# Routed pairs of a mixture-of-experts stage: both up halves ahead of the down product of the preceding pair, and VectorE's weighing behind both gated products

## What is computed

```python
def swiglu(x, w1, w2, w3):
    h = x @ w1
    return h * jax.nn.sigmoid(h) * (x @ w2) @ w3
...
top_v, top_i = jax.lax.top_k(gate_out, TOP_K)
...
out = jax.vmap(one_expert, in_axes=(0, 0, 0, 2))(ew1, ew2, ew3, w).sum(0)
out = out + swiglu(x, sw1, sw2, sw3)
...
h = h + _L0_ffn_ref(_layernorm(h, axis=-1), ...)
```

## Time and profile before

| | us |
|---|---|
| median of 3 runs (lowest to highest) | 1470.19 (1468.88 to 1470.64) |
| the profiled execution, its own time | 1476.68 |
| span of the profiled execution, first to last instruction | 1474.9 |
| PE busy in that span | 1277.8 (87%) |
| DVE busy | 1043.0 (71%) |
| ACT busy | 831.4 (56%) |
| POOL busy | 960.0 (65%) |

### The profile page before, as it was taken

The page is one execution under the profiler, slowest core; times in us unless marked ns, Lnnn a source line. Parts: engine busy times, 40 slices in busy tenths (PEclk is TensorE's granted clock), DMA queues, the critical chain, the costliest instruction groups (busy, mean ns, idle before and its releaser), DMA issues. The chain is left out here.

```text
span 1474.9 us, 37041 instructions
## 1 busy us (share of the span) xinstructions
PE 1277.8 (87%) x10992; PEld 1053.6 (71%) x10993; DVE 1043.0 (71%) x2675; ACT 831.4 (56%) x2286; POOL 960.0 (65%) x958
## 2 busy tenths in 40 slices
PE   4400499999999999999999999879989999999996
PEld 3400388888888888888888888645557888788884
DVE  3245789998998899899889999756564444444442
ACT  1230388778778877787787777765632322222221
POOL 0057789889889888988898889558640333333333
PEclk8755799999999999999999999979999999999998
DMA  9993264543463355346332546554433434444440
GB/s 320 380 319 118 47 127 102 138 87 69 102 133 64 64 131 108 64 89 142 70 65 58 116 87 107 97 84 127 128 125 102 67 54 58 70 57 58 63 60 8
DMA packets 354415, 157.13 MB, mean 107 GB/s; under 512 B 283953, under 2 KB 338737, under 8 KB 354353
## 3 DMA queue, kind: packets, MB, share of 16 engines
q1 hardware_dynamic: 321090, 117.99, 35.8%
q0 software_dynamic: 20064, 25.32, 9.3%
q10 hardware_dynamic: 13200, 13.11, 2.5%
HBM read 44.50 MB, written 42.64 MB: 59 GB/s over the span
## 5 line engine op out<-in xcount | busy, mean ns | idle before, releaser
L731 PE MATMUL bank<-hT,Wc 128*128 128x256 f16 x2304 | 285.8, 274 | 88.0 <-DMA hT<-hhl 76.0
L731 PEld LDWEIGHTS bank<-hT,Wc 128*128 128x128 f16 x2304 | 226.7, 98 | 115.9 <-issue 88.5
L691 POOL DMA_INDIRECT out_rows<-h0b,payin x78 | 121.5, 1557 | 235.4 <-DVE h0b L1471 182.8
L828 PE MATMUL bank<-xTg,Wall 128*128 128x256 f16 x1872 | 211.1, 273 | 0.0
L828 PEld LDWEIGHTS bank<-xTg,Wall 128*128 x1872 | 183.2, 98 | 21.4
L1096 ACT ACTIVATE silu<-bank 128x512 f32<-128x512 f32 x110 | 65.6, 596 | 215.0 <-PE bank L828 177.0
L596 POOL TENSOR_TENSOR h0b<-h0b,rows 128x512 f32<-128x512 f32 x96 | 121.9, 1269 | 98.0 <-issue 52.6
L1399 DVE SCALAR_TENSOR_TENSOR gT<-bank,silu 128x512 f32<-128x512 f32 x110 | 76.0, 691 | 130.2 <-ACT silu L1096 124.3
L731 PE MATMUL bank<-Wc,MT 128*128 128x256 f16 x1152 | 143.3, 275 | 9.8 <-DVE MT L1262 9.8
L731 PE MATMUL bank<-khl,eqT 128*128 128x256 f16 x1152 | 142.4, 274 | 6.0 <-DVE khl L1274 0.3
L731 PE MATMUL bank<-Wc,hT 128*128 128x256 f16 x1152 | 142.0, 273 | 0.0
(11 more groups left out here) (150 smaller groups left out, 2585.8 us busy)
## 6 DMA issues: line engine op xcount, KB each, us to landing
Wall<-in_L_tok_W SPq DMA_DIRECT2D x25, 512.0 KB, 7.8
emb_rows<-Wall ACTq DMA_DIRECT2D x25, 512.0 KB, 11.7
Wall<-in_L_ffn_ew SPq DMA_DIRECT2D x24, 512.0 KB
Wc<-Wn SPq DMA_DIRECT2D x48, 128.0 KB
Wst<-in_L_attn_w_qkv SPq DMA_DIRECT2D x12, 384.0 KB
h_rows<-Wall SPq DMA_DIRECT2D x4, 1024.0 KB, 4.4
X<-h_rows POOLq DMA_DIRECT2D x8, 512.0 KB, 6.6
out_rows<-X SPq DMA_DIRECT2D x8, 512.0 KB
```

The costliest lines, as they stand in the source:

```text
L691: pool.indirect_dma_start(out=out_rows, out_offset=bass.IndirectOffsetOnAxis(ap=got(j % PAYS, w, 0, i32), axis=0), in_=yout[j % 2][:, w, : ...
L731: last = mm(to, lhs(a, k, o), moving, start=(i == 0 and k == 0), stop=(i == 2 and k == 1))
L828: last = mm(to, cols(a, e, 2 * k + w, (2 * half + c) * P, P), moving, start=(n_ == 0), stop=(n_ == 5))
```

## The change

Two statements change places in the PE stream and two in the DVE stream. No instruction is added or taken away, and the streams of ACT, POOL and SP are the same.

```diff
@@ PE, round_ @@
                     up_slots(j, p, 0, at[i], nth[i // 2])
-                    if prev is not None:
-                        down(pair[i] + SHP, 1 - p, prev)
-                    else:
+                    if prev is None:
                         down_shared(SHP - 2)
                     up_slots(j, p, 1, at[i], nth[i // 2])
                     if prev is None:
                         down_shared(SHP - 1)
+                    else:
+                        down(pair[i] + SHP, 1 - p, prev)
                     prev = at[i]
@@ DVE @@
             for j in range(1, PAIRS):
                 gate(SHP + j, 0)
+                gate(SHP + j, 1)
                 weigh(j - 1, 1 - j % 2, (j - 1) % PAYS, (j - 1) // PAYS + 1)
-                gate(SHP + j, 1)
             weigh(PAIRS - 1, 0, (PAIRS - 1) % PAYS, (PAIRS - 1) // PAYS + 1)
```

## The result

The changed kernel took 1446.79 us (median of 4 runs, 1444.24 to 1448.58) against 1470.41 us for the kernel before in the same comparison (4 runs as well): a ratio of 0.9843, 95% interval 0.9827 to 0.986, so 23.6 us faster. The profiled execution took 1447.14 us, with a span of 1445.4 us.

The account below looks back on a forecast made before the run. PE, at 8.516 us a pair, was held by waits for a gating chain longer than its cover; -28.5 us at PE's end plus 2.8 given back made -25.7, so 1470.19 became 1444.5 us, range 1440.5 to 1450.

Parts of the forecast that it names:

- a chain of 2.85 us: Gating on ACT and DVE, from SiLU to the down product that uses its low part: 2.85 us.
- a cover of 2.62 us: The one block of 24 up matmuls PE has between u(j,1) and d(j) in the old order: 2.62 us.
- 7.86 us a pair: Pair loop on PE: three blocks without waits cost 7.86 us a pair, instead of 8.516.
- the run-out: Block ahead of each stop ends in full instead of being overlapped: 0.16 us, to go away with the wait.
- the slow start: Block behind each stop takes 2.91 to 2.93 us against 2.78, some 0.14 us, to go away with the wait.
- The rival of 1456 us: Pair loop: only the named idle goes, as changing block kind costs the rest; 14.1 us gained, chance 0.07.
- PE's end: Last down product, d(38): stop of some 0.25 us, then 2.90 us, ending at 1435.6 instead of 1464.16, 28.5 us earlier.
- The end's queue: Program end on POOL: pair 38's scatters wait for pair 37's to land, giving back 2.8 us.
- the bounds that I gave: Program end: time given back lies between 0 (pair 37's scatters early enough) and 5.1 us (landing takes 3.5).
- The rival that round starts show: PE's sequencer loading experts stalls PE up to 0.5 us at six round starts: 3 us, 1447.5, chance 0.08.
- POOL as the next bound: Scatters in the pair loop: POOL's period of 7.69 us is below 7.86, so it keeps up.
- The slow rival: POOL becomes the bound: scatters landing in 4.5 us make its period 8.70 us, total 1477, chance 0.02.

Follow-up runs that it names:

- the shorter chain: Kernel before, with the low part of half 1 computed for only 32 of 512 columns: 1452.96 us against 1471.24.
- a longer chain: Changed kernel with the low part of half 1 computed twice in a row: 1450.96 us against 1474.1 for the kernel before.
- the longer chains: Low part of half 1 computed twice: in the kernel before 1503.67 us, in the changed kernel 1450.96, both against 1474.1.
- more work on POOL: Changed kernel with one 128 x 512 float32 addition on POOL before each pair's scatters: 1450.12 us against 1471.92 for the kernel before.

## Why the prediction was right

**What bounds the kernel: shown.** I held that in each pair the path leaves PE because a chain of 2.85 us stands against a cover of 2.62 us. Lengthening the chain cost 28 us in the old order and 0.7 us in the new one, and shortening it in the old order gave 18.3 us.

**7.86 us a pair: shown, to the hundredth,** and with it the claim that not only the idle time of 15 us goes but also the run-out and the slow start around each stop. The rival of 1456 us, only the named idle, is refuted: the pair stretch fell by 25.3 us. Two readings were less exact. The idle time before a down product was 0.27 to 0.43 us and not only the 0.27 to 0.33 that I named; its mean of 0.35 makes the excess of 0.656 us add up (0.35, 0.16 and 0.14). And "both go away with the wait" is true of the run-out only: with the shorter chain the idle time and the run-out were gone and the slow start stayed. In the change it went because the wait is met some 5 us ahead.

**PE's end: right.** I put the start of the last down product 2.85 us behind the end of u(38,1), at the price of 2.90 us. It stood 2.89 us behind, a stop of 0.27 us, and took 2.97 us at a granted clock of 1.00.

**The end's queue: right.** 2.8 us given back was worked out from a landing of 1.2 us, read at the very last scatter, and a restart of 0.78, read behind DVE; no row showed either for a scatter that waits for another. Measured from the end of u(38,1) the program ended 19.3 us later in the forecast (1449.2 - 1429.87) and 1445.4 - 1426.05 = 19.35 us in the trace. POOL went on 2.00 us behind its last issue, against 1.98. There was some luck in it. The median scatter of the changed kernel lands 3.8 us after the start of its issue, so 2.2 us behind its end; had pair 37's landed like that and not after 1.2 us, the end would have come 1 us later, inside the bounds that I gave.

**The sum.** The stretch from u(0,1) on was to be 1449.2 - 1128.41 = 320.8 us and is 321.2. The 0.4 us are the late starts at four rounds. The rival that round starts show was half right, a gap at four of them, of 0.04 to 0.11 us and not 0.5. I had argued from the seven starts without a gap in the trace of before. Why that order shows none, where a stop stands one block behind each round start, was not tried.

**The time.** Forecast 1444.5 us, measured 1446.79 and, in a later comparison, 1446.13 against 1471.24. I subtracted a difference of 25.7 us from a median; the medians differ by 23.6 (95% interval 20.6 to 25.4), 25.1 and, with a longer chain, 23.1. The runs spread by 4.3 us. That this comes from the part ahead of the pairs is likely but not shown: only two of these executions were profiled, and their pair stretches agree to 0.1 us.

**POOL as the next bound: not reached, but closer than I wrote.** I took 0.78 us as the start behind DVE and argued from one period of 7.69 us that POOL keeps up. It does, with a room of at least 1.2 us. The slow rival, a landing of 4.5 us, has no support: scatters landed 2.7 to 4.7 us after the start of an issue of 1.56 us, so 3.1 us behind its end at most. An issue took up to 1.98 us there, not always 1.55 to 1.56, and nothing waited for it. That the late weighing costs nothing in the loop is shown by the PE order alone beside the whole change: with either order of DVE the new PE order has its 7.86 us.

**The transposing loads** landed in 3.2 to 5.2 us (4.5 at most before) against a cover of 10.5, and no wait for them appeared.

The Trainium skill's figure for a DMA issued by GpSimd (DMA: Bandwidth & Descriptors, on the anatomy of such a DMA) would have put the end 0.8 us earlier. The trace has 1438.23 to 1440.9, when SP goes on, 2.7 us from issue to landing, as in the row of before and not the page's 2.3, and 2.7 is the shortest of its 78 scatters (median 3.8); the measurement decides.

## What to carry to other kernels

When an engine waits a little in every turn for a chain on other engines, compare the chain's length with the work that stands between its start and its use, and reorder so that one more block stands between: the gain is more than the idle time in the waits, because each stop also costs a run-out and a slow start. Aim for a wait that is met well ahead of its turn: met 0.23 us ahead, the down product still had its slow start here. Then follow the last turn by itself, since a queue that never mattered in the loop (here POOL's landing) decides there. And a step that a single consumer needs late, like the tables on DVE, belongs behind the work that the bounding engine waits for.

## What the runs showed that I had not expected

**PE stops without a releaser in some executions of the same code.** In the shared stage, which the change doesn't touch, the timeline of PE of the kernel before shows stops for which no engine is to blame ("issue"). Some of its rows:

```profile
1028.01 0.17 PE L792 MATMUL bank<-gwp,xT 128*128 128x8 f16 x1 [0.50 <-issue]
1028.73 0.23 PE L792 MATMUL bank<-gwp,xT 128*128 128x8 f16 x3 [0.55 <-issue]
1030.14 0.18 PE L792 MATMUL bank<-gwp,xT 128*128 128x8 f16 x1 [1.19 <-issue]
1030.18 4.44 PE L859 MATMUL bank<-xT,Wall 128*128 128x512 f16 x12
1042.74 0.61 PE L876 MATMUL bank<-Wall,gThl 128*128 128x256 f16 x4 [0.44 <-issue]
1058.91 1.81 PE L876 MATMUL bank<-Wall,gThl 128*128 128x256 f16 x15 [0.43 <-issue]
1076.23 1.81 PE L876 MATMUL bank<-Wall,gThl 128*128 128x256 f16 x15 [0.43 <-issue]
```

There are eight of them for 4.1 us, and the 12 matmuls behind the longest took 4.44 us where they take 2.75 elsewhere; the granted clock from 1020 to 1040 us was 0.91, and 1.00 in the changed kernel. The profiled executions with the PE order alone, the DVE order alone and the longer chains have them too, at nearly the same places; those of the changed kernel (both), the shorter chain and all later runs have none. The four runs with them shared a chip; whether the chip, the build or chance decides was not tried. The 4.25 us between the two starts of u(0,1) arise here: the same matmuls stand 0.06 us apart in the two traces at 998.6 us and 4.9 us apart at 1077.9. It is not a simple sum, as the executions without these stops wait 2.6 to 3.1 us for low parts of the shared expert in their place (L1410; 0.2 us in the kernel before), and one without them still started u(0,1) at 1126.26 (more work on POOL).

**A scatter starts late on GpSimd, an addition does not.** It takes 0.78 us from the end of what releases it to the start of a scatter, behind DVE and even behind GpSimd's own addition, and some 0.8 us behind the landing of the scatters before. But the addition on the same engine started 0.14 us behind DVE. So the late start belongs to the indirect DMA and not to GpSimd. On DVE and ACT the step from one to the other takes 0.03 us.
